# Attention with routed experts on one core: query and output products of most pairs in three passes of high and low parts

## The chip, the cores and the metric

One NeuronCore of a Trainium2 chip runs the whole program. The metric is the device time of one launch in microseconds, lower is better. 0.5% of it is 2.3 us.

## What is computed

The reference is a layer of cross attention followed by a routed feed-forward layer, for 2 sequences of 1024 tokens with 256 features and a context of 154 keys:

```
x = x + attention(layernorm(x), ctx)        # 16 heads of 16; q = xn Wq + bq, k, v from ctx
                                            # concat(softmax(q k^T / 4) v) Wo + bo
x = x + experts(layernorm(x))               # 8 experts, the best 2 per token, weighted by
                                            # softmax of the router's logits; gelu, 256 -> 1024 -> 256
```

All data is float32. The router's choice of 2 from 8 hangs on the attention's result, so products are kept at full or nearly full float32 accuracy.

## The kernel before

The 2048 tokens are 16 tiles of 128 rows, taken two at a time as 8 **pairs** (`MACROS = 8`, `PAIR = 256` columns). The attention stage is a software pipeline written out by hand: each engine has its own program of steps m = 0 to 7 (`step`, `quiet_step` for the last two, `QUIET = 6`, `LAST = 7`), and runs it strictly in that order; engines meet at semaphores (`wait_ge`, `then_inc`). In step m TensorE computes the scores of pair m + 2 (for their maxima), the scores of pair m again with keys on the partitions (`turned_scores`, ten per pair), the value sums, back transposes, head transposes and output product of pair m - 1, the router of pair m - 2, and the transposes and query product of pair m + 4. A pair's way through the engines:

- `statistics1` on VectorE and `next_norm1` on GpSimd normalise it; `xn_transposes` (L1441) turns it into a PSUM bank, `evac_xnT` on ScalarE (L654) copies it to `xnT`, `q_product` (L1450) multiplies by `wq_sb` into the same bank, `evac_q` (L661, L669) scales it and makes the rounded high part, `low_queries` on GpSimd (L487) the low part. Both go through DRAM (`qd`) into `QS` by DMAs that SP writes and GpSimd's queue reads (`queries_read`, L505).
- `scores` (L1483), `maxima` on VectorE (L1004), `negatives` (L1015, L1017), `maxima_transposes` (L1498). From pair 3 on these transposes wait until the residual sums of two pairs earlier are made.
- `turned_scores` (L1529, L1532), `exp` on ScalarE (L684), `value_sums` (L1555, L1557), `back_transposes` (L1567), `normalise` on VectorE (L1023, L1027), `head_transposes` (L1574) into `ps_a`, `evac_heads` on ScalarE (L696) to `OT`, `wo_product` (L1583) once per tile, `add_residual` on VectorE (L1037), `statistics2`, `norm2` on GpSimd, the transposes and `router`.

A `turned_scores` waits for the exponential two before it, since there are two banks. In step 1 VectorE and ScalarE also lay out the keys of the second sequence (`low_keys`, L978; `high_keys`, L732). In steps 6 and 7 the maxima are done, and VectorE starts on the routing: `places`, `slots_of` (L1211, L1213) and `lanes_of` (L1204) for the first 8 tiles in step 6, `choose(1)` and `sum_up(1)` (L1164 to L1261) for tiles 8 to 11 in step 7. These stand ahead of `add_residual`. On TensorE `ranks(1)` (L1621 to L1626) waits for `sum_up(1)` and stands ahead of the value sums of the last pair; `value_sums` of pair 6 wait for the first residual sum of pair 5.

Two kinds of products occur. On float32 tiles the multiplication is at full accuracy; on tiles of the 4-byte rounded type (`f32r`) one pass is made on rounded operands, and accuracy comes from splitting an operand into a rounded high part and the rounded rest. The expert stage does so already (`up`, L1832, three passes), with VectorE making low parts (L1361). `q_product` and `wo_product` are of the first kind:

```
last = mm(query_bank(m)[:, g * PAIR:(g + 1) * PAIR], wq_sb[:, c, g * P:(g + 1) * P],
          xnT[:, c, :], start=c == 0, stop=c == KC - 1)
```

## Time and profile before

| | |
|---|---|
| median of 3 runs | 454.18 us (453.14 to 455.15) |
| the profiled execution | 454.41 us, its span 452.5 us |
| busy over the span | TensorE 88%, weight loads 74%, VectorE 62%, ScalarE 51%, GpSimd 44% |
| mean granted TensorE clock | 0.944 |
| attention stage, routing, expert stage | to about 190 us, to about 210 us, to the end |

The profile is that of one execution. Times inside it are counted from the start of the span; engines other than the one that is looked at work at the same time. A TensorE record's duration is modelled and overlaps the next one's, so what a product costs is read from the chain of waits, where pieces don't overlap, or from the distance of starts. PEclk is the granted clock as a share of 2.4 GHz. In the rows below PE is TensorE, PEld its weight loads, DVE is VectorE, ACT ScalarE, POOL GpSimd.

### The profile page before, as it was taken

What the parts mean: (1) busy time and instruction counts of PE and PEld (TensorE: products, weight loads), DVE (VectorE), ACT (ScalarE), POOL (GpSimd) and SP (SyncE); (2) the same over time, 40 slices, a digit from 0 to 9 for tenths busy, and PEclk for the clock granted to TensorE, in tenths of its full rate; (3) what the DMA queues carried; (4) which work ended last, traced back from release to release, by engine and by line L of the source; (5) the groups of instructions that cost most, each with busy time, mean ns of one, the idle gap of its engine ahead of it and who ended that gap; (6) DMA issues with size and microseconds to landing.
All of it is one profiled execution on the core that took longest, in us unless ns stands there. A gap on an engine that the chain in (4) does not pass through costs nothing.

```text
span 452.5 us, 8680 instructions
## 1 busy us (share of the span) xinstructions
PE 400.3 (88%) x2742; PEld 334.0 (74%) x2743; DVE 279.1 (62%) x655; ACT 229.1 (51%) x420; POOL 199.8 (44%) x183
## 2 busy tenths in 40 slices
PE   6967798999999998658899999999999989999950
PEld 2645665768668665535899999999999979999940
DVE  2898848456475657786976646644468865744320
ACT  1653647456454664241756456544457755644420
POOL 4846567372632322006235363255434664452230
PEclk9895999999998999858999999999999999999995
DMA  8446553433610110753554542723227732232220
GB/s 236 138 101 138 120 118 80 97 97 73 167 40 16 54 48 30 252 172 94 219 182 102 180 62 56 212 48 50 44 47 220 215 65 48 44 54 30 25 29 12
DMA packets 25750, 45.39 MB, mean 100 GB/s; under 512 B 6512, under 2 KB 19952, under 8 KB 22960
## 3 DMA queue, kind: packets, MB, share of 16 engines
q0 software_dynamic: 8448, 15.77, 19.2%
q1 hardware_dynamic: 13760, 26.32, 18.3%
q10 hardware_dynamic: 3504, 2.83, 2.0%
q8 instruction: 20, 0.33, 0.3%
q14 instruction: 18, 0.15, 0.1%
HBM read 31.52 MB, written 13.39 MB: 99 GB/s over the span
## 4 chain that ended last, share of the span: by engine, by line
PE 69%; DVE 12%; DMA 5%; issue 4%; ACT 3%; POOL 1%; POOLq 0%; ACTq 0%; DVEq 0%
PE ps_s L1832 20%; PE ps_t L1849 14%; PE ps_t L1852 7%; DMA result<-big,rowtok 4%; DVE mx L1004 3%; PE ps_s L1483 3%; PE ps_t L1532 2%; PE ps_a L1557 2%; PE ps_c L1557 2%; PE ps_a L1555 2%; PE ps_c L1814 2%; PE ps_t L1529 2%; DMA big<-rows,gtok 2%; PE ps_c L1555 2%; PE ps_c L1450 1%
## 5 line engine op out<-in xcount | busy, mean ns | idle before, releaser
L1832 PE MATMUL ps_s<-xgT,KB 128*128 128x256 f32 x912 | 110.8, 280 | 3.0 <-DVE xgT L1361 3.0
L622 POOL DMA_INDIRECT result<-big,rowtok x38 | 63.6, 1673 | 111.4 <-DMA result<-big,rowtok 61.0
L1832 PEld LDWEIGHTS ps_s<-xgT,KB 128*128 128x128 f32 x912 | 108.5, 188 | 4.2 <-DVE xgT L1361 1.7
L1004 DVE TENSOR_REDUCE mx<-ps_s 128x4 f32<-128x616 f32 x64 | 49.4, 797 | 31.7 <-PE ps_s L1483 31.5
L590 POOL DMA_INDIRECT big<-rows,gtok x38 | 44.9, 1181 | 32.7 <-DVE gtok L1318 14.9
L1849 PE MATMUL ps_t<-KB,HTb 128*128 x160 | 56.9, 397 | 0.0
L684 ACT ACTIVATE big<-ps_t 128x512 f32<-128x512 f32 x80 | 45.3, 593 | 21.9 <-PE ps_t L1532 18.2
L1849 PE MATMUL ps_t<-KB 128*128 x144 | 51.9, 402 | 0.0
L876 ACT ACTIVATE big<-ps_t,wrow 128x256 f32<-128x256 f32 x38 | 18.1, 477 | 65.8 <-PE ps_t L1852 60.7
L1377 DVE TENSOR_TENSOR HTb<-big,HTb 128x512 fp32r<-128x512 f32 x40 | 27.6, 692 | 31.7 <-ACT big L868 31.6
L868 ACT ACTIVATE big<-ps_s 128x512 f32<-128x512 f32 x76 | 45.4, 597 | 0.0
L1852 PE MATMUL ps_t<-KB,HTb 128*128 x160 | 44.7, 280 | 0.0
L1852 PE MATMUL ps_t<-KB 128*128 x144 | 40.4, 281 | 0.0
L1377 DVE TENSOR_TENSOR KB<-big,KB 128x512 fp32r<-128x512 f32 x36 | 24.7, 692 | 24.7 <-ACT big L868 23.1
L1483 PE MATMUL ps_s<-KB 96*128 96x308 f32 x128 | 33.6, 356 | 6.2 <-DVE mx L1004 2.9
L452 POOL TENSOR_TENSOR mv<-mv,half_sb 128x2 f32<-128x2 f32 x15 | 11.1, 743 | 62.2 <-DVE mv L1048 45.0
L866 ACT ACTIVATE HTb<-ps_s 128x512 fp32r<-128x512 f32 x40 | 24.0, 601 | 26.1 <-PE ps_s L1832 23.9
L1409 DVE SCALAR_TENSOR_TENSOR big<-ps_t,wrow,big 128x256 f32<-128x256 f32 x38 | 17.8, 482 | 30.2 <-ACT big L876 21.6
L1849 PEld LDWEIGHTS ps_t<-KB,HTb 128*128 128x128 f32 x160 | 30.1, 188 | 6.6 <-issue 0.2
L1532 PE MATMUL ps_t<-KB 100*128 100x256 f32 x128 | 29.6, 327 | 4.2 <-ACT big L684 3.9
L1849 PEld LDWEIGHTS ps_t<-KB 128*128 128x128 f32 x144 | 27.1, 188 | 6.2
L1483 PEld LDWEIGHTS ps_s<-KB 96*128 96x128 f32 x128 | 21.5, 207 | 12.9 <-DVE mx L1004 6.2
(234 smaller groups left out, 714.2 us busy)
## 6 DMA issues: line engine op xcount, KB each, us to landing
VP<-in_wexp SPq DMA_DIRECT2D x8, 1024.0 KB
big<-in_wexp SPq DMA_DIRECT2D x8, 1024.0 KB
qd<-big SPq DMA_DIRECT2D x28, 128.0 KB, 2.3
KB<-qd POOLq DMA_DIRECT2D x7, 512.0 KB, 5.2
result<-x SPq DMA_DIRECT2D x8, 256.0 KB, 2.9
rows<-xn SPq DMA_DIRECT2D x8, 256.0 KB, 2.9
KB<-qd POOLq DMA_DIRECT2D x7, 256.0 KB, 5.4
XS<-in_x ACTq DMA_DIRECT2D x1, 1024.0 KB, 5.5
```

The costliest lines, as they stand in the source:

```text
L590: pool.indirect_dma_start(XG[:, n, :], None, rows, bass.IndirectOffsetOnAxis(gtok[:, n:n + 1], 0)).then_inc(xg_loaded[u % 2], 16)
L622: pool.indirect_dma_start(out, bass.IndirectOffsetOnAxis(rowtok[:, u, h:h + 1], 0), ys[:, 2 * (u % 2) + h, :], None, compute_op=ALU.add).t ...
L684: act.activation(dst, ps_t[(n + 1) % 2][:, :].rearrange("p (h n) -> p h n", h=2), ACT.Exp).then_inc(p_made, 1)
L866: act.activation(hidT[u % 2][:, 0, 2 * b:2 * b + 2, :], ps_s[b // 2][:, b % 2, :].rearrange("p (j n) -> p j n", j=2), ACT.Gelu)
L868: act.activation(hid[:, b, :], ps_s[b // 2][:, b % 2, :], ACT.Gelu).then_inc(hid_made, 1)
L1004: dve.tensor_reduce(mx[:, i, :, 2 * k:2 * k + 2].rearrange("p a b -> p b a"), ps_s[n % 2][:, :, 0:2 * KEYS].rearrange("p b (h k) -> p b h ...
L1377: dve.tensor_tensor(hidT[u % 2][:, 1, js, :], hid[:, b, :].rearrange("p (j n) -> p j n", j=2), hidT[u % 2][:, 0, js, :].bitcast(fp32), ALU ...
L1483: last = mm(ps_s[n % 2][:, j, 0:2 * KEYS], QS[0:96, u, p, i * P:(i + 1) * P], KS[0:96, b, p, :], start=True, stop=True)
L1532: last = mm(bank[:, h, :], KS[0:100, b, place(j - 2), h * KEYS:h * KEYS + P], QS[0:100, u, place(j - 2), :], start=True, stop=True)
L1832: last = mm(ps_s[j // 4][:, j // 2 % 2, (j % 2) * PAIR:(j % 2 + 1) * PAIR], w1[:, w, k, j * P:(j + 1) * P], xgT[:, u % 2, a, k, :], start= ...
L1849: mm(ps_t[h][:, :].rearrange("p (w d) -> p w d", w=2), hidT[u % 2][:, 0, j, half_rows], w2[:, bass.ds(par, 1), :, j, :].squeeze(1), start= ...
L1852: last = mm(ps_t[h][:, 0:D], hidT[u % 2][:, 1, j, half_rows], w2[:, bass.ds(par, 1), 0, j, :].squeeze(1), start=False, stop=j == HJ - 1, s ...
```

## The change

Three things. The weights `wo_sb` and `wq_sb` are split once into a rounded high part and a rounded rest, by GpSimd, early in the program. For pairs 4 to 7 of the query product and pairs 0 to 6 of the output product, ScalarE's copy out of PSUM now writes the rounded part, VectorE subtracts it from the same bank to make the low part (`low_xnT`, `low_heads`), and TensorE makes three passes: high by high, high by low, low by high. The remaining pairs are as before. The new tiles lie in `HTb`, which the expert stage uses later. And the order is changed at four places: `turned_scores(m, 5)` ahead of the query product, `exp(m, 5)` ahead of `evac_q`, in step 1 `high_keys(1, 2)` with it, and in steps 6 and 7 `turned_scores` 8 and 9 each one place forward, ahead of an output product. The diff, without declarations of semaphores:

```diff
@@ -134,6 +134,10 @@
+        HTb = sb("HTb", [P, HT], f32r)
+        OT2, xnT2, wo2, wq2 = (HTb[:, 1024 * n:1024 * n + 1024].rearrange("p (s c n) -> p s c n", s=2, c=KC) for n in range(4))
+        THREE = ((0, 0), (0, 1), (1, 0))
...
@@ -549,11 +554,19 @@
             low_queries(1)
+            pool.wait_ge(ld_w, 48)
+            pool.tensor_copy(wo2[:, 0, :, :], wo_sb[:, :, :]).then_inc(wo2_hi, 1)
+            pool.wait_ge(wo2_hi, 1)
+            pool.tensor_tensor(wo2[:, 1, :, :], wo_sb[:, :, :], wo2[:, 0, :, :].bitcast(fp32), ALU.subtract).then_inc(wo2_made, 1)
             queries_read(1)
             low_queries(2)
             next_norm1(3)
             queries_read(2)
             maxima_read(0)
+            pool.wait_ge(ld_q, 16)
+            pool.tensor_copy(wq2[:, 0, :, :], wq_sb[:, :, :]).then_inc(wq2_hi, 1)
+            pool.wait_ge(wq2_hi, 1)
+            pool.tensor_tensor(wq2[:, 1, :, :], wq_sb[:, :, :], wq2[:, 0, :, :].bitcast(fp32), ALU.subtract).then_inc(wq2_made, 1)
             next_norm1(4)
             low_queries(3)
...
@@ -651,7 +664,7 @@
-                act.activation(xnT[:, :, :], query_bank(m)[:, :].rearrange("p (c n) -> p c n", c=KC), ACT.Copy).then_inc(xnT_made, 1)
+                act.activation((xnT if m < RING else xnT2[:, 0, :, :])[:, :, :], query_bank(m)[:, :].rearrange("p (c n) -> p c n", c=KC), ACT.Copy).then_inc(xnT_made, 1)
@@ -693,7 +706,7 @@
-                act.activation(OT[:, :, :], ps_a[:, :].rearrange("p (g n) -> p g n", g=GROUPS), ACT.Copy).then_inc(OT_made, 1)
+                act.activation(OT2[:, 0, :, :], ps_a[:, :].rearrange("p (g n) -> p g n", g=GROUPS), ACT.Copy).then_inc(OT_made, 1)
@@ -821,6 +834,10 @@
                     exp(m, 4)
                 if m == 1:
                     high_keys(1, 0)
+                if has(0):
+                    exp(m, 5)
+                if m == 1:
+                    high_keys(1, 2)
                 if has(4):
                     evac_q(m + 4)
...
                 if has(0):
-                    for j in range(5, 10):
+                    for j in range(6, 10):
                         exp(m, j)
-                        if m == 1 and j in (5, 7):
-                            high_keys(1, (j - 1) // 2)
+                        if m == 1 and j == 7:
+                            high_keys(1, 3)
@@ -1026,6 +1043,16 @@
+            def low_xnT(m):
+                dve.wait_ge(xnT_made, m + 1)
+                dve.tensor_tensor(xnT2[:, 1, :, :], query_bank(m)[:, :].rearrange("p (c n) -> p c n", c=KC),
+                                  xnT2[:, 0, :, :].bitcast(fp32), ALU.subtract).then_inc(xnT_lo, 1)
+
+            def low_heads(m):
+                dve.wait_ge(OT_made, m + 1)
+                dve.tensor_tensor(OT2[:, 1, :, :], ps_a[:, :].rearrange("p (g n) -> p g n", g=GROUPS),
+                                  OT2[:, 0, :, :].bitcast(fp32), ALU.subtract).then_inc(OT_lo, 1)
@@ -1119,7 +1146,11 @@
                 if has(5):
                     statistics1(m + 5)
+                if has(4):
+                    low_xnT(m + 4)
                 for n in range(5, 8):
+                    if n == 7 and has(-1):
+                        low_heads(m - 1)
                     if has(2):
                         maxima(m + 2, n)
@@ -1445,8 +1476,16 @@
             def q_product(m, gs=range(GROUPS)):
                 if 0 in gs:
                     pe.wait_ge(xnT_made, m + 1)
+                    if m >= RING:
+                        pe.wait_ge(xnT_lo, m - RING + 1)
+                        pe.wait_ge(wq2_made, 1)
                 for g in gs:
                     for c in range(KC):
+                        if m >= RING:
+                            for k, (a, w) in enumerate(THREE):
+                                last = mm(query_bank(m)[:, g * PAIR:(g + 1) * PAIR], wq2[:, w, c, g * P:(g + 1) * P],
+                                          xnT2[:, a, c, :], start=c == 0 and k == 0, stop=c == KC - 1 and k == 2)
+                            continue
@@ -1579,7 +1618,15 @@
                 pe.wait_ge(OT_made, m + 1 + i * int(m == LAST))
...
+                if m < LAST:
+                    pe.wait_ge(OT_lo, m + 1)
+                    pe.wait_ge(wo2_made, 1)
                 for g in range(GROUPS):
+                    if m < LAST:
+                        for k, (a, w) in enumerate(THREE):
+                            last = mm((ps_a, ps_c)[i][:, 0:D], OT2[:, a, g, i * P:(i + 1) * P], wo2[:, w, g, :],
+                                      start=g == 0 and k == 0, stop=g == GROUPS - 1 and k == 2)
+                        continue
@@ -1723,10 +1770,10 @@
                 turned_scores(m, 7)
+                turned_scores(m, 8)
                 wo_product(m - 1, 0)
-                turned_scores(m, 8)
+                turned_scores(m, 9)
                 wo_product(m - 1, 1)
-                turned_scores(m, 9)
@@ -1773,10 +1820,10 @@
+                if has(0):
+                    turned_scores(m, 5)
                 if has(4):
                     q_product(m + 4)
-                if has(0):
-                    turned_scores(m, 5)
```

In step 3 TensorE's part from the head transposes (L1574, in the new program L1613) to the last scores of keys, before:

```order
L1574 MATMUL ps_a<-id_sb,heads 128x128 x4
L1532 MATMUL ps_t<-KB 128x256 x2
L1483 MATMUL ps_s<-KB 128x308 x2
L1450 MATMUL ps_c<-xnT,wq_sb 128x256 x4
L1529 MATMUL ps_t<-KB 128x256 x4
L1483 MATMUL ps_s<-KB 128x308 x2
L1583 MATMUL ps_a<-wo_sb,OT 128x256 x2
L1532 MATMUL ps_t<-KB 128x256 x2
L1583 MATMUL ps_c<-wo_sb,OT 128x256 x2
L1532 MATMUL ps_t<-KB 128x256 x6
```

and now, where the query product's three passes are L1486, the output product's L1627, and the scores of keys L1568 and L1571:

```order
L1613 MATMUL ps_a<-id_sb,heads 128x128 x4
L1571 MATMUL ps_t<-KB 128x256 x2
L1522 MATMUL ps_s<-KB 128x308 x2
L1568 MATMUL ps_t<-KB 128x256 x4
L1486 MATMUL ps_c<-HTb 128x256 x12
L1522 MATMUL ps_s<-KB 128x308 x2
L1627 MATMUL ps_a<-HTb 128x256 x6
L1571 MATMUL ps_t<-KB 128x256 x2
L1627 MATMUL ps_c<-HTb 128x256 x6
L1571 MATMUL ps_t<-KB 128x256 x6
```

The scores with the two key remainders (x4) have moved ahead of the query product, whose 4 products became 12; each output product went from 2 to 6.

VectorE in step 7, from the heads' normalisation (L1023, L1027) over the copy of the logits (L1110) to the first operations of the choice, before:

```order
L1023 RECIPROCAL rec<-ps_a 128x16
L1027 TENSOR_TENSOR heads<-ps_a,rec 128x256
L1023 RECIPROCAL rec<-ps_c 128x16
L1027 TENSOR_TENSOR heads<-ps_c,rec 128x256
L1110 COPY LG<-ps_s 128x16
L1164 TENSOR_REDUCE r_m<-LG 128x4
L1165 TENSOR_TENSOR r_b<-LG,r_m 128x32
L1166 TENSOR_TENSOR r_b<-r_b,em_sb 128x32
L1167 TENSOR_REDUCE r_c<-r_b 128x4
```

and now (L1040, L1044, L1137, and the choice from L1195 on):

```order
L1040 RECIPROCAL rec<-ps_a 128x16
L1044 TENSOR_TENSOR heads<-ps_a,rec 128x256
L1040 RECIPROCAL rec<-ps_c 128x16
L1044 TENSOR_TENSOR heads<-ps_c,rec 128x256
L1137 COPY LG<-ps_s 128x16
L1054 TENSOR_TENSOR HTb<-ps_a,HTb 128x512
L1195 TENSOR_REDUCE r_m<-LG 128x4
L1196 TENSOR_TENSOR r_b<-LG,r_m 128x32
L1197 TENSOR_TENSOR r_b<-r_b,em_sb 128x32
L1198 TENSOR_REDUCE r_c<-r_b 128x4
```

The subtraction for the low part of the heads (L1054) stands between the copy of the logits and the choice of the experts, ahead of all of it.

TensorE in the same step, from the head transposes to the rank products (L1621 to L1626), before:

```order
L1574 MATMUL ps_a<-id_sb,heads 128x128 x4
L1532 MATMUL ps_t<-KB 128x256 x2
L1583 MATMUL ps_a<-wo_sb,OT 128x256 x2
L1532 MATMUL ps_t<-KB 128x256 x2
L1583 MATMUL ps_c<-wo_sb,OT 128x256 x2
L1532 MATMUL ps_t<-KB 128x256 x2
L1621 MATMUL ps_s<-r_pick,before_bf 128x32
L1623 MATMUL ps_s<-r_sum_bf,ones_bf 128x32
L1626 MATMUL ps_s<-r_pick,ones_bf 128x24
L1626 MATMUL ps_s<-r_pick,ones_bf 128x16
L1626 MATMUL ps_s<-r_pick,ones_bf 128x8
```

and now (rank products L1668 to L1673):

```order
L1613 MATMUL ps_a<-id_sb,heads 128x128 x4
L1571 MATMUL ps_t<-KB 128x256 x4
L1627 MATMUL ps_a<-HTb 128x256 x6
L1571 MATMUL ps_t<-KB 128x256 x2
L1627 MATMUL ps_c<-HTb 128x256 x6
L1668 MATMUL ps_s<-r_pick,before_bf 128x32
L1670 MATMUL ps_s<-r_sum_bf,ones_bf 128x32
L1673 MATMUL ps_s<-r_pick,ones_bf 128x24
L1673 MATMUL ps_s<-r_pick,ones_bf 128x16
L1673 MATMUL ps_s<-r_pick,ones_bf 128x8
```

One score of keys has moved ahead of each output product; the rank products still come behind both.

## Rows read from the trace of the kernel before

**Rows 1.** Page, part 1: busy us (share of the span) xinstructions

```profile
PE 400.3 (88%) x2742; PEld 334.0 (74%) x2743; DVE 279.1 (62%) x655; ACT 229.1 (51%) x420; POOL 199.8 (44%) x183
```

**Rows 2.** Windows: us, PE, PEld, DVE, ACT, POOL busy (x), PEclk, DMA share, GB/s

```profile
96.30:114.50 18.20, 17.44 (x129) 13.40 (x127) 10.29 (x22) 9.93 (x19) 7.36 (x8) 1.00 0.42 103
...
130.90:148.90 18.00, 17.13 (x117) 13.03 (x115) 11.09 (x30) 8.29 (x15) 7.53 (x7) 0.91 0.11 34
...
72.00:77.00 5.00, 3.51 (x18) 2.22 (x17) 4.81 (x13) 4.78 (x9) 2.56 (x3) 1.00 0.28 70
...
77.00:80.70 3.70, 3.70 (x22) 1.27 (x21) 0.68 (x1) 0.22 (x1) 3.54 (x4) 0.54 0.43 131
...
142.00:145.70 3.70, 3.70 (x18) 3.64 (x18) 2.09 (x4) 1.77 (x4) 0.00 (x0) 0.54 0.00 0
```

**Rows 3.** Chain of waits in order of time: start us, us, what

```profile
108.64 1.73 PE ps_c L1450 x8
...
127.56 0.87 PE ps_a L1583 x4
...
162.14 0.43 PE ps_a L1555 x2
...
174.99 0.03 PE ps_s L1621
...
227.94 5.63 PE ps_s L1832 x48
```

**Rows 4.** One line's instructions: duration ns min/median/max, first and last start us, forms

```profile
L1361 DVE TENSOR_TENSOR xgT<-ps_c,xgT x19: 690/691/693, 210.2 to 413.0; 128x512 fp32r<-128x512 f32 x19
...
L519 POOL CAST KB<-big x4: 603/607/742, 17.8 to 19.8; 32x512 fp32r<-32x512 f32 x4
...
L487 POOL TENSOR_TENSOR big<-qf,big x8: 1257/1272/1499, 16.2 to 112.0; 128x512 fp32r<-128x512 f32 x8
```

**Rows 5.** Timeline of GpSimd, start: start us, us, line, operation [idle before <-releaser]

```profile
29.99 0.80 POOL L505 DMA_DIRECT2D KB<-qd  x1 [4.39 <-DMA qd<-big]
...
42.08 0.72 POOL L452 TENSOR_TENSOR mv<-mv,half_sb 128x2 f32<-128x2 f32 x1 [2.14 <-DVE mv L936]
```

**Rows 6.** Timeline of ScalarE, step 4

```profile
126.31 0.60 ACT L696 ACTIVATE OT<-ps_a 128x512 f32<-128x512 f32 x1 [0.65 <-PE ps_a L1574]
```

**Rows 7.** Timeline of VectorE and GpSimd, steps 0, 1 and 4

```profile
52.50 1.50 DVE L1004 TENSOR_REDUCE mx<-ps_s 128x4 f32<-128x616 f32 x2
...
73.29 1.26 POOL L487 TENSOR_TENSOR big<-qf,big 128x512 fp32r<-128x512 f32 x1
...
73.39 1.21 DVE L1017 SCALAR_TENSOR_TENSOR nm<-mx,nm 128x32 fp32r<-128x32 f32 x1
...
75.14 0.42 DVE L1037 TENSOR_TENSOR x<-ps_a,XS 128x256 f32<-128x256 f32 x1
...
128.65 0.19 DVE L1017 SCALAR_TENSOR_TENSOR nm<-mx,nm 128x32 fp32r<-128x32 f32 x1
```

**Rows 8.** Timeline of GpSimd, step 3

```profile
112.05 1.28 POOL L487 TENSOR_TENSOR big<-qf,big 128x512 fp32r<-128x512 f32 x1 [8.80 <-ACT big L669]
```

**Rows 9.** Timeline of VectorE, step 4

```profile
126.83 1.56 DVE L1004 TENSOR_REDUCE mx<-ps_s 128x4 f32<-128x616 f32 x2 [0.17 <-PE ps_s L1483]
```

**Rows 10.** Timeline of ScalarE and VectorE, step 6

```profile
158.29 0.28 DVE L1211 TENSOR_TENSOR o_code<-r_o,pick_code 128x128 f16<-128x128 f32 x1
...
159.03 0.59 ACT L696 ACTIVATE OT<-ps_a 128x512 f32<-128x512 f32 x1
...
159.06 1.23 DVE L1204 TENSOR_TENSOR XS<-count_sb,lane_f 128x1024 f16<-128x1024 f32 x1
```

**Rows 11.** Timeline of VectorE and ScalarE, step 7

```profile
171.25 0.19 DVE L1164 TENSOR_REDUCE r_m<-LG 128x4 f32<-128x32 f32 x1
...
171.87 0.59 ACT L696 ACTIVATE OT<-ps_a 128x512 f32<-128x512 f32 x1
...
174.55 0.17 DVE L1261 CAST r_sum_bf<-r_sum 128x8 bf16<-128x8 f32 x1
```

More of the change, by code:

```diff
@@ L210, in xattn_moe_kernel @@
         hid = big[:, o5:o5 + HID * 2].rearrange("p (b n) -> p b n", b=4)
-        HTb = sb("HTb", [P, HT], f32r)
         hidT = [part.rearrange("p (s j n) -> p s j n", s=2, j=HJ)
@@ L246, in xattn_moe_kernel @@
         v_psum, v_made = sem("v_psum"), sem("v_made")
+        xnT_lo, OT_lo, wo2_hi, wo2_made, wq2_hi, wq2_made = (sem(n) for n in
+            ("xnT_lo", "OT_lo", "wo2_hi", "wo2_made", "wq2_hi", "wq2_made"))
         st1_made, mv1_made, var1_made, rstd1_made = (sem(n) for n in ("st1_made", "mv1_made", "var1_made", "rstd1_made"))
```

## The prediction

> **What bounds the kernel now.** The change lies in the attention stage (before 190 us), so I began with the page's totals and went on to the stretches of that stage. Over the span TensorE is busy 88%, VectorE 62% [rows 1]: on average VectorE has room. By steps (step m scores pair m, prepares pairs m + 1 to m + 5 and finishes pairs m - 1 and m - 2) TensorE is busy 17.44 of 18.20 us in step 3 and 17.13 of 18.00 in step 5 [rows 2]. It sets the pace, and it waits for a few tenths wherever a result of ScalarE or VectorE is just in time. Twice its granted clock is down at half (1.2 of 2.4 GHz) for some 3.7 us: the rows 77 to 80.7 and 142 to 145.7 show a mean of 0.54 [rows 2]. Each costs up to 1.8 us. The chain of waits runs through TensorE nearly without a break; so an instruction that TensorE loses is a gain only if nothing else comes late, and a late operand is a loss at its full length.
>
> **Products.** A 4-byte product of 256 columns is two records of 0.216 us: the query product (4 products) 1.73 us, one output product (2 products) 0.87 us [rows 3]. A product of rounded operands is one record: 48 of them take 5.63 us, 0.117 each, with the same 128x128 weights and 256 columns [rows 3]. New query product: 12 x 0.117 = 1.41, 0.32 less, four times: -1.3 us. New output product: 6 x 0.117 = 0.70, 0.17 less, fourteen times: -2.3 us. Full credit would be **-3.6 us**.
> The Trainium skill (FP8 and Floating Point Precision, TensorE Precision Notes) counts a true FP32 product as four passes through the array. Three of four would be 1.30 and 0.65 us, and -4.8 us in all; the rows speak for less, since a pass that is an instruction of its own takes 0.117 and not 0.108.
>
> **ScalarE** writes the rounded part in place of the 4-byte copy: same shape, same 0.6 us [rows 6], nothing.
>
> **GpSimd splits the weights.** A cast of 512 elements a lane takes 0.60 to 0.74 us, a subtraction of two SBUF tiles 1.26 to 1.50 [rows 4]: 1.9 to 2.2 us per split. The first stands where GpSimd idles 4.39 us for a transfer, the second where it idles 2.14 us for VectorE [rows 5]. Both are covered; the second just so, and what is queued behind it (the norm of pair 4, then pair 3's low query part) has more than a microsecond left. I take 0 and keep +0.7 as the upper end: a cast that gets in ahead of VectorE's first norm would hold it that long.
>
> **VectorE's low parts.** Eleven subtractions, PSUM minus SBUF, 128x512, rounded on output. The nearest row is the same operation of the expert stage: 0.69 us [rows 4]. VectorE works in its program's order, so their cost is where they stand and what is queued behind them. I go step by step.
> Steps 0 and 1 are already full on VectorE. In step 0 the low part stands in front of the maxima that ran at 52.50 [rows 7]; it ends at about 53.2, TensorE wanted the query product at 52.4 (the moved scores of keys cover 0.5), so the product ends 1 us later. ScalarE's exponential 5, now ahead of the query evacuation, gives most of it back: **+0.2**. In step 1 1.4 us are added to a VectorE that is busy 4.81 of the 5 us from 72 to 77 [rows 2]. Before, 1.0 us of it was lost anyway: L1017 took 1.21 us, where it takes 0.19 in step 4, until GpSimd's L487 had ended [rows 7]. But two low parts push the third key copy (L978) into the same stretch of GpSimd; it then waits in L1017's place, and itself, L1015, L1017, the last copy still stand between it and the residual sum. That sum moves from 75.14 to about 76.0, and the transposes of the maxima wait for it: **+0.9** (0.1 if GpSimd comes second).
> The Trainium skill (SBUF — State Buffer, Who interferes with whom) says that a copy or cast in a two-port mode, or an operation with two SBUF inputs against a reading GpSimd, waits for the whole instruction of the other, while one with a single SBUF input does not. L1017 agrees. By it the new subtractions themselves stay at 0.69 beside GpSimd, and it is the copies around them that pay.
> Step 2: the query product waits 0.3 for its low part and the output product 0.4, against 0.65 saved; ScalarE, with the last key copies, is the bound at the end: **+0.1**. Step 3 has no statistics, and both low parts come in time. TensorE saves 0.65, but with the scores moved ahead the query product ends when it did, so GpSimd's L487 still starts at 112.05 and ends at 113.33 [rows 8]; L1017 waits for that as before, and the residual sum behind it holds the next transposes: **-0.2**.
> Step 4 has no query product. ScalarE's copy of the turned heads ends at 126.91 [rows 6], but VectorE was taking the last two maxima of the step, 126.83 to 128.39 [rows 9]; the low part goes between them, 127.6 to 128.3. TensorE was at the output product at 127.56 [rows 3]; it now starts at 128.35 with its first weight load not covered (0.2). Loss 1.0, less 2 x 0.17 saved: **+0.65**. Step 5 is the same, but in this execution half its work ran at half clock, which gave VectorE time: **+0.4**.
> Step 6: the scores of keys put ahead of the output product cover the low part (copy ends 159.62, low part 160.3). Behind it on VectorE stand the slot tables and the lane table (0.7 + 1.23 us), which ran from 158.29 to 160.29 while the heads were under way [rows 10]. Now they run from 160.35 to 162.4, then comes the residual sum of pair 5, 162.75, and the next value sums wait for it; they began at 162.14 [rows 3]: **+0.7**.
> Step 7 is the largest. VectorE chose the experts of tiles 8 to 11 from 171.25 to 174.72, 17 small operations without a gap [rows 11], in the shadow of ScalarE's copy at 171.87 and of the output products. The low part now stands ahead of them and can't start before 172.46, when the copy ends; it ends at 173.16. The choice ends at 173.2 + 3.47 = 176.65. TensorE's rank products wait for its sum, and the value sums of the last pair are queued behind them. They started at 174.99, with 0.2 us in hand [rows 3]; now at 176.8: **+1.8**. Nothing later has slack for it up to the first expert product.
> Sum: 0.2 + 0.9 + 0.1 - 0.2 + 0.65 + 0.4 + 0.7 + 1.8 = **+4.55 us**. The profiled execution took 454.41 us (span 452.5); that makes 459.0. The median of the three runs is 454.18, so the sum would be 458.7 against it; I stay with 459.0. The expert stage is untouched.
>
> **The range.** Adding the lower ends (start 0, steps 0, 0.1, -0.2, -0.5, 0.5, 0, 0.5, 1.7) gives +2.1, the upper ones (0.7, then 0.5, 1.0, 0.4, 0, 0.8, 0.7, 0.8, 2.0) +6.9. One stretch of half clock less or more moves either end by 1.8: 454.7 to 463.1, of which I keep 454.7 to 462.5, since all upper ends together are unlikely.
>
> **Rivals.**
> (1) *The passes pay in full.* If the new waits all fall into time in which TensorE would wait anyway, the -3.6 us stand, less a little: 451 us. For it: TensorE is the bound in steps 3 to 5. Against it: the ends of the copies and the starts of the products are in the rows, and step 7's 17 operations have nowhere to go. The point from which it decides is where the low part ends before TensorE has reached the output product; only step 3 is there. Chance 0.08.
> (2) *The clock stays up.* If both stretches of half clock disappear, since the work of steps 1 and 5 falls otherwise, 3.6 us come back: 4.55 - 3.6, 455.4, within 0.5%. For it: in the rows it went down after stretches with short waits, and other steps with such waits kept it. Chance 0.14.
> (3) *The new waits bring more half clock.* In step 7 TensorE would stand still for nearly 2 us and then start the value sums. Before the drop at 77 it had stood still 1.5 of 5 us, in pieces [rows 2]. One to two stretches more give +1.8 to +3.6: 461 to 462.6. Chance 0.14.
> The Trainium skill (TensorE: Matmul & The Clock Gate, What's actually happening) has the throttled state as the default that activity releases; that is on the side of (3).
> (4) *The change does not do what it says*, the products not taking the one-record form: then twelve records would be 24 and the query product 5.2 us; since the tiles are declared in the same type as those of rows 3, I give it nothing of its own.
>
> **Chances.** The queue losses of the sum as they stand 0.64, (3) 0.14, (2) 0.14, (1) 0.08. A measurement of this kernel can tell about 0.5%, 2.3 us, from no change: slower is above 456.5, faster below 451.9. The sum's own case falls below 456.5 in one of ten. Slower 0.58 + 0.14 + a little of (2) = 0.76, same 0.17, faster 0.07. The range 454.7 to 462.5 leaves out (1), the far end of (3) and a little of (2), some 0.17.
>
> **What would show it.** Right: output product records of half the length, near 0.28 busy with 0.117 between them; TensorE waits for the new VectorE line ahead of the output product of pairs 3 and 4, about 0.8 us each; in step 7 a gap of nearly 2 us ahead of the rank products, released by VectorE's sum; the value sums of pair 6 starting on the residual sum. Wrong: no gap there, or the new VectorE line at more than 0.8 us, or an expert stage that starts no later than now.

## The result and the profile after

The changed kernel takes 458.24 us, median of five runs (457.81 to 459.24); the kernel before, beside it, 453.25 (452.39 to 455.15). The ratio is 1.0103, with a 95% interval of 1.0067 to 1.0139: 3.0 to 6.3 us slower. Forecast were 459.0 and "slower". The profiled execution of the changed kernel took 458.24 us with a span of 456.3. Medians here are of all runs; the ratios, and the fit further down, leave out nine of 207 runs that were over 1.5% slower than the fastest of their kernel.

Page of the changed kernel, part 1, against [rows 1]:

```profile
PE 401.4 (88%) x2786; PEld 335.5 (74%) x2787; DVE 282.7 (62%) x666; ACT 229.0 (50%) x420; POOL 206.5 (45%) x187
```

VectorE has its eleven instructions and GpSimd its four; TensorE is as busy as before over the span. That sum hides what happened in the steps, so the next thing to read is a window for each step, against [rows 2]: steps 4 and 5, the old place of half clock at 142, and the two new ones. The first line is step 4 of the kernel before, the others are the changed kernel.

```profile
114.40:130.80 16.40, 15.53 (x117) 11.45 (x115) 10.12 (x25) 8.19 (x16) 7.13 (x11) 1.00 0.46 114
...
114.00:131.10 17.10, 15.43 (x120) 11.38 (x118) 10.24 (x24) 8.17 (x16) 7.12 (x11) 1.00 0.49 112
131.10:148.30 17.20, 15.55 (x121) 11.47 (x120) 11.56 (x31) 8.27 (x16) 7.52 (x7) 1.00 0.11 35
142.00:145.70 3.70, 2.87 (x21) 2.65 (x22) 3.54 (x5) 2.01 (x4) 0.00 (x0) 1.00 0.00 0
159.90:163.60 3.70, 3.66 (x16) 3.43 (x16) 2.41 (x5) 1.03 (x4) 0.00 (x0) 0.55 0.01 2
187.20:190.90 3.70, 3.25 (x8) 2.00 (x6) 2.63 (x12) 0.00 (x0) 0.57 (x1) 0.55 1.00 407
```

In step 4 TensorE is busy 15.43 us instead of 15.53, but the step takes 17.1 us instead of 16.4: what was added is waiting. The granted clock (third number from the end) fell to half in other places than before: near 58, at 159.9 and at 187.2, and no longer at 77 and 142. So step 5 looks faster than before (17.14 against 17.99) and step 6 looks slower than it is.

Timeline of TensorE in the changed kernel, the new products:

```profile
52.80 1.66 PE L1486 MATMUL ps_c<-HTb 128*128 128x256 f32 x12 [0.69 <-issue]
...
74.26 0.95 PE L1627 MATMUL ps_a<-HTb 128*128 128x256 f32 x6 [1.54 <-DVE HTb L1054]
...
127.96 0.95 PE L1627 MATMUL ps_a<-HTb 128*128 128x256 f32 x6 [0.78 <-issue]
128.75 0.40 PE L1571 MATMUL ps_t<-KB 100*128 100x256 f32 x2
128.98 0.87 PE L1627 MATMUL ps_c<-HTb 128*128 128x256 f32 x6
129.69 0.52 PE L1571 MATMUL ps_t<-KB 100*128 100x256 f32 x3
...
177.16 0.19 PE L1668 MATMUL ps_s<-r_pick,before_bf 128*128 128x32 bf16 x1 [0.80 <-DVE r_pick L1207]
177.20 0.18 PE L1670 MATMUL ps_s<-r_sum_bf,ones_bf 128*128 128x32 bf16 x1
```

From the chain of waits of the changed kernel, against L1450 and L1583 in [rows 3]:

```profile
52.80 1.67 PE ps_c L1486 x12
...
109.33 1.44 PE ps_c L1486 x12
...
111.05 0.72 PE ps_a L1627 x6
...
127.96 0.95 PE ps_a L1627 x6
```

In step 3, where TensorE doesn't wait, a query product takes 1.44 us in the chain instead of 1.73, an output product 0.72 instead of 0.87: the credit of 0.3 and 0.15 is there, at about 0.12 us a pass. Behind a wait it is gone or nearly so: the query product of step 0 takes 1.67 us and the first output product of step 4 takes 0.95 (the forecast had 0.2 us there for a first weight load that nothing covers). Ahead of the first output product of steps 4 to 7 stands an idle time of 0.76 to 0.78 us, in step 1 one of 1.54. "issue" in the timeline doesn't say whom it waited for; the end of VectorE's low part does:

```profile
23.09 2.04 DVE L1084 TENSOR_SCALAR xn<-XS,mv 128x256 f32<-128x256 f32 x2
...
52.01 0.68 DVE L1049 TENSOR_TENSOR HTb<-ps_c,HTb 128x512 fp32r<-128x512 f32 x1
...
74.75 0.99 DVE L995 CAST KB<-big 32x616 fp32r<-32x616 f32 x1
...
76.72 0.42 DVE L1064 TENSOR_TENSOR x<-ps_a,XS 128x256 f32<-128x256 f32 x1
...
127.18 0.68 DVE L1054 TENSOR_TENSOR HTb<-ps_a,HTb 128x512 fp32r<-128x512 f32 x1
...
159.15 0.69 DVE L1054 TENSOR_TENSOR HTb<-ps_a,HTb 128x512 fp32r<-128x512 f32 x1 [1.28 <-ACT HTb L709]
...
160.53 1.22 DVE L1235 TENSOR_TENSOR XS<-count_sb,lane_f 128x1024 f16<-128x1024 f32 x1
161.67 0.42 DVE L1064 TENSOR_TENSOR x<-ps_a,XS 128x256 f32<-128x256 f32 x1
...
173.68 0.69 DVE L1054 TENSOR_TENSOR HTb<-ps_a,HTb 128x512 fp32r<-128x512 f32 x1 [1.28 <-ACT HTb L709]
174.28 0.17 DVE L1195 TENSOR_REDUCE r_m<-LG 128x4 f32<-128x32 f32 x1
...
176.92 0.18 DVE L1207 TENSOR_TENSOR r_pick<-r_o 128x32 bf16<-128x32 f32 x1
...
177.59 0.17 DVE L1292 CAST r_sum_bf<-r_sum 128x8 bf16<-128x8 f32 x1
```

This is VectorE of the changed kernel in the start and in steps 0, 1, 4, 6 and 7. 127.18 + 0.68 is 127.86, and the product starts at 127.96. In step 7 VectorE stands idle for 1.28 us for ScalarE's copy, does the low part, and only then begins the choice of the experts (at 174.28; in [rows 11] the choice began at 171.25, ahead of the copy). Its picks are ready at 177.10, and the rank products start at 177.16.

### The profile page after: what moved, and what is told of

Read it like the earlier page. It is cut to its first block, busy times and chain, and to the rows that moved or that the text cites. A ratio compares the mean times of both kernels' runs of the same rounds, so it can differ in the third digit from the quotient of the medians.

```text
span 456.3 us, 8801 instructions
## 1 busy us (share of the span) xinstructions
PE 401.4 (88%) x2786; PEld 335.5 (74%) x2787; DVE 282.7 (62%) x666; ACT 229.0 (50%) x420; POOL 206.5 (45%) x187
## 4 chain that ended last, share of the span: by engine, by line
PE 64%; DVE 10%; DMA 9%; issue 6%; POOL 4%; ACT 3%; ACTq 0%; SPq 0%; DVEq 0%; POOLq 0%
PE ps_s L1879 18%; PE ps_t L1896 12%; PE ps_t L1899 6%; PE ps_s L1522 3%; DMA big<-rows,gtok 3%; PE ps_t L1571 3%; DMA result<-big,rowtok 2%; DVE mx L1021 2%; PE ps_a L1596 2%; PE ps_a L1594 2%; PE ps_t L1568 2%; PE ps_c L1596 2%; PE ps_t L1457 2%; PE ps_c L1594 2%; PE ps_c L1861 2%
## 5 line engine op out<-in xcount | busy, mean ns | idle before, releaser
L635 POOL DMA_INDIRECT result<-big,rowtok x38 | 64.6, 1699 | 108.7 <-DMA result<-big,rowtok 63.2
L603 POOL DMA_INDIRECT big<-rows,gtok x38 | 46.9, 1235 | 33.1 <-DVE gtok L1349 14.6
L1896 PEld LDWEIGHTS ps_t<-KB,HTb 128*128 128x128 f32 x160 | 30.0, 188 | 6.3 <-issue 0.2
L1571 PE MATMUL ps_t<-KB 100*128 100x256 f32 x128 | 27.1, 309 | 3.7 <-ACT big L697 3.7
L1899 PEld LDWEIGHTS ps_t<-KB,HTb 128*128 128x128 f32 x160 | 30.2, 189 | 0.0
```

Of the source, the lines that this page charges most:

```text
L603: pool.indirect_dma_start(XG[:, n, :], None, rows, bass.IndirectOffsetOnAxis(gtok[:, n:n + 1], 0)).then_inc(xg_loaded[u % 2], 16)
L635: pool.indirect_dma_start(out, bass.IndirectOffsetOnAxis(rowtok[:, u, h:h + 1], 0), ys[:, 2 * (u % 2) + h, :], None, compute_op=ALU.add).t ...
L1571: last = mm(bank[:, h, :], KS[0:100, b, place(j - 2), h * KEYS:h * KEYS + P], QS[0:100, u, place(j - 2), :], start=True, stop=True)
L1896: mm(ps_t[h][:, :].rearrange("p (w d) -> p w d", w=2), hidT[u % 2][:, 0, j, half_rows], w2[:, bass.ds(par, 1), :, j, :].squeeze(1), start= ...
L1899: last = mm(ps_t[h][:, 0:D], hidT[u % 2][:, 1, j, half_rows], w2[:, bass.ds(par, 1), 0, j, :].squeeze(1), start=False, stop=j == HJ - 1, s ...
```

## The lengths of the steps

To follow one step through many kernels I measured in every profile from the first maxima transpose of one step to that of the next; step 6 ends at the value sums of pair 6, step 7 at the rank products. A number with * has 3.2 to 3.4 us at half clock in it, which lengthens it by up to half of that. The lengths of the other experiments stand in their text.

| step | before | before again | after | order only | no low parts | low parts early | low part ahead of maxima 6 | low part in the middle |
|---|---|---|---|---|---|---|---|---|
| 0 | 11.85 | 11.86 | 12.24 | 11.62 | 11.35 | 11.35 | 12.26 | 13.50* |
| 1 | 18.52 | 19.17 | 20.20* | 18.03 | 18.88 | 19.78 | 20.58* | 18.63 |
| 2 | 20.15* | 20.09* | 18.81 | 18.44 | 19.64* | 19.57* | 18.81 | 18.82 |
| 3 | 18.17 | 18.14 | 17.56 | 18.17 | 17.59 | 17.55 | 17.57 | 17.57 |
| 4 | 16.43 | 16.42 | 17.14 | 16.42 | 17.69* | 16.53 | 16.55 | 18.31* |
| 5 | 17.99* | 16.43 | 17.14 | 16.43 | 17.65* | 17.69* | 16.55 | 17.16 |
| 6 | 13.20 | 13.21 | 14.80* | 12.97 | 12.65 | 13.49 | 13.97 | 13.48 |
| 7 | 12.85 | 12.86 | 14.09 | 12.62 | 12.29 | 13.04 | 14.08 | 13.03 |

Where no half clock is in it and GpSimd doesn't collide with VectorE (all but step 1), a step of the same work repeats to 0.04 us from profile to profile. The totals don't: the runs of the kernel before spread from 450.6 to 460.0 us, and about two thirds of that variance goes with the granted clock. I therefore also fitted 198 runs by least squares with one constant for each kernel and one price, the same for all kernels, for a microsecond at half clock. That price came out at 0.26 us (+-0.02), and the constants, all at 45 us of half clock, stand with the experiments as "at equal clock" (standard error 0.3 to 0.5 us, 0.1 for before): 454.1 for before, 457.5 for after.

## The experiments

My theory: each loss is a place in VectorE's queue, and moves with the low part. The rivals: the order moves or GpSimd's weight splits cost the time; or the clock does, and then nothing done to the queue gives it back. Each kernel below has 6 to 12 runs, but for the repeat of before, which has one. The kernel before took 454.69 us beside one to four, 453.73 beside five to eight and 455.99 beside nine to twelve.

**One: the last two steps as before** (three passes for the output products of pairs 0 to 4 only, and the scores of steps 6 and 7 in their old order).

```
+        WIDE = 5
...
-                if m < LAST:
+                if m < WIDE:
                     pe.wait_ge(OT_lo, m + 1)
```

> Steps 6 and 7 as in the kernel before (4-byte output products of pairs 5 and 6, old order, no low part on VectorE there); steps 0 to 5 as changed. Theory (low parts stand in VectorE's queue ahead of routing work): the stretch from the maxima transposes of step 5 to the rank products of step 7 falls back from 28.9 to about 26.1 us, and the whole to 455.5 to 456.5 us against 458.2 of the change. Rival (the loss comes from steps 0 to 5 or from half clock alone): stays at 457.5 to 458.5.

Measured: 458.23 us, ratio 1.0088 (1.0054 to 1.0121); at equal clock 456.4, 1.1 under the change. Steps 6 and 7 came back to 13.21 and 12.86, those of before. The total missed my expectation and lies where the rival had it. The profile shows 17.1 us at half clock before step 0 where the change had 13.7, which at the fitted price is 0.9 us; the steps speak for the queue, the total alone for neither.

**Two: the query products alone** (no output product in three passes; the scores of steps 6 and 7 in their old order).

```
+        WIDE = 0
...
-                if m < LAST:
+                if m < WIDE:
                     pe.wait_ge(OT_lo, m + 1)
```

> Only the query products of pairs 4 to 7 in three passes; all output products 4-byte, no low part of the heads; both weights still split by GpSimd, order of steps 0 to 3 as changed. Theory: the query side is nearly even (steps 0 and 1 lose some tenths, step 3 gains 0.3), 453.0 to 454.5 us against 453.3 before. Rival (weights' split and the query side carry a good part of the loss): 455 to 456 us.

Measured: 457.86 us, ratio 1.0051 (1.0014 to 1.0089); at equal clock 455.0. Steps 4 and 5 are 16.43 and 16.43 again. The total is above both expectations, with on average 51 us at half clock against 47 for before, and step 1 took 21.95 us with 6.8 at half clock.

**Three: the low part of pair 5 between slot tables and lane table, that of pair 6 in the middle of the choice.**

```
                     slots_of(0)
+                    low_heads(m - 1)
                     lanes_of(0, 0)
...
+                if n == 1:
+                    low_heads(LAST - 1)
```

> As the change, but in step 6 the low part of the heads stands between slot tables and lane table, in step 7 in the middle of the choice of the experts. Theory: VectorE no longer stands idle for the copy (1.28 us twice); the picks are 0.7 us late, within the slack of 0.9 us that TensorE had there, so the gap ahead of the rank products goes, 1.2 us less in step 7 and 0.3 to 0.7 in step 6: 456.3 to 457.0 us. Rival (the passes and the low part's own 0.69 us are what costs): 457.8 to 458.5.

Measured: 457.86 us, ratio 1.0075 (1.0047 to 1.0103); at equal clock 457.0. Step 6 fell from 13.97 (its length without half clock, in four) to 13.48, step 7 from 14.09 to 13.03. The total is above what I expected, in the rival's range. TensorE waits for the low part just as long, but the gap ahead of the rank products is gone:

```profile
176.73 0.95 PE L1630 MATMUL ps_a<-HTb 128*128 128x256 f32 x6 [0.76 <-issue]
...
178.46 0.19 PE L1671 MATMUL ps_s<-r_pick,before_bf 128*128 128x32 bf16 x1
```

The gap of 0.80 us ahead of the rank products was due to what is queued behind the low part.

**Four: in steps 4 and 5 the low part ahead of the last two maxima.**

```
-                    if n == 7 and has(-1):
+                    if n == (6 if m in (4, 5) else 7) and has(-1):
```

> As the change, but in steps 4 and 5 the low part of the heads stands ahead of maxima 6 and not behind them. Theory: it ends 0.6 to 0.7 us earlier, TensorE's wait ahead of the output product (0.78 us) shrinks to 0.1 to 0.2, steps 4 and 5 take 16.5 us in place of 17.1: 1.2 us less, 457.0 us. Rival (ScalarE's exponentials bound these steps anyway): no change, 458.2.

Measured: 458.43 us, ratio 1.0115 (1.0066 to 1.0163); at equal clock 457.2. Steps 4 and 5 fell from 17.14 to 16.55. Its TensorE timeline has 0.18 us where 0.78 stood:

```profile
127.78 0.96 PE L1627 MATMUL ps_a<-HTb 128*128 128x256 f32 x6 [0.18 <-issue]
```

The total didn't show the 1.2 us of the two steps: the median is that of the change, where I expected 457.0, and at equal clock only 0.3 of them appear, with an error of 0.5 us on either kernel. In the steps the low part's place is shown to cost 0.6 us each; in the total it can't be told.

**Five: all low parts early** (the places of three; in steps 1 to 5 the place of four; and the low query part ahead of the statistics).

```
-                if has(5):
-                    statistics1(m + 5)
                 if has(4):
                     low_xnT(m + 4)
                 for n in range(5, 8):
-                    if n == 7 and has(-1):
+                    if n == 6 and has(-1) and m < QUIET:
                         low_heads(m - 1)
+                    if n == 7 and has(5):
+                        statistics1(m + 5)
```

> The change with every low part placed where VectorE has room: low_xnT ahead of statistics1, low_heads of steps 1 to 5 ahead of the maxima of strip 6, the one of step 6 between the slot tables and the lane table, the one of step 7 in the middle of the choice of the experts. My theory (each loss is a queue position on VectorE) expects steps 4 and 5 at 16.5 us instead of 17.1, the stretch of step 6 at 13.5 and that of step 7 at 13.0, the start of step 0 to step 1 no longer than 12.2 and step 1 at 18.5 to 19.2 without half clock, so 2.5 to 3 us less than the change at the same clock: 455 to 456.5. The rival that the loss sits in the clock, not in the queue, expects the same shorter steps and a total within 1 us of the change, with more us at half clock. The rival that the passes pay in full once nothing is late expects 451 to 452.

Measured: 456.28 us, ratio 1.0046 (1.0016 to 1.0076); at equal clock 455.1, 2.4 (+-0.6) less than the change. The steps are as expected but for step 1 (19.78). Most of the loss at equal clock is gone, at the same three passes, the same eleven subtractions and the same splits. The rival "the passes pay in full" found no support: with the low parts at these better places the kernel is still no faster than before. In one, three, four and five the totals at equal clock give back 1.1, 0.5, 0.3 and 2.4 us of the 2.0, 1.5, 1.2 and about 3.7 that their steps became shorter (steps 1 and 2 left out, and step 5 of five taken like step 4). All four are counted from the same five runs of the change, with an error of 0.5 us, so whether a part is lost again elsewhere stays open.

**Six: the weight splits alone** (before, plus GpSimd's four instructions; nobody reads what they write).

```
             low_queries(1)
...
+            pool.tensor_copy(wo2[:, 0, :, :], wo_sb[:, :, :]).then_inc(wo2_hi, 1)
...
+            pool.tensor_tensor(wo2[:, 1, :, :], wo_sb[:, :, :], wo2[:, 0, :, :].bitcast(fp32), ALU.subtract).then_inc(wo2_made, 1)
...
             maxima_read(0)
...
+            pool.tensor_copy(wq2[:, 0, :, :], wq_sb[:, :, :]).then_inc(wq2_hi, 1)
```

> The kernel before plus GpSimd's two weight splits alone; what they write is read by nobody, everything else is as before. My theory (the splits stand in GpSimd's idle time) expects no difference: 0 to 0.3 us, the maxima transposes of step 0 at 45.2 to 45.7 at the same clock, steps 0 and 1 at 11.85 and 18.5. The rival (the casts hold VectorE in the start, or the clock goes down for longer there) expects 0.7 to 3 us more, with the transposes of step 0 at 46.4 to 48.6, as three of the five kernels with splits showed.

Measured: 455.96 us, ratio 1.0030 (0.9996 to 1.0064); at equal clock 454.3, 0.2 over before. Nothing can be told from no change. All steps are within 0.03 us of those of before.

**Seven: three passes only where they gained** (query pairs 6 and 7, output pairs 1 and 2, which are steps 2 and 3; in these steps the low parts stand at the places of five, and all other steps have their old order; the splits stay early).

```
+        Q3, O3 = (6, 7), (1, 2)
...
-                        if m >= RING:
+                        if m in Q3:
```

> Three passes only where the traces show room on VectorE: query products of pairs 6 and 7 and output products of pairs 1 and 2, which fall into steps 2 and 3, with the order of those steps as in the change and of all others as before. My theory expects steps 0 and 1 as before (11.85 and 18.5), step 3 at 17.5 (0.6 less), step 2 at about 18.5 (0 to 0.3 less than its clean value), the rest as before: 0.6 to 1.2 us faster than before, 453. The rival that any three-pass product brings more time at half clock expects no gain, 454 to 456, with over 3 us more at half clock.

Measured: 453.09 us beside 453.73 for before, ratio 0.9951 (0.9914 to 0.9987); at equal clock 452.3. Step 3 is 17.55 and steps 4 to 7 are those of before. This is the one version that comes out ahead of the kernel before, by the ratio 0.5%. Its interval only just leaves out 1, the two medians are 0.6 us apart, and the same products with the splits elsewhere (nine) are no faster than before, so the 0.6 us of step 3 are sure and the total is not.

**Eight: the kernel before again**, for a second profile.

> The kernel before itself, for a second profile: the lengths of its steps where the clock falls elsewhere. Both theories expect a span of 450.5 to 455.5; step 1 at 18.5 and step 3 at 18.17 again if these are the clean values, and step 2 and step 5 at 18.3 to 18.5 and 16.4 to 16.5 if they are free of half clock this time.

Measured: 453.08 us, span 451.1. Step 5 is 16.43 without half clock, so [rows 2] had 1.56 us of clock in it. Step 1 is 19.17 us with no half clock either, 0.65 more than the first time: its length is not fixed even for one kernel.

**Nine: as seven, with the weight splits behind the low queries of pairs 3 and 4.**

```
             low_queries(3)
+            pool.wait_ge(ld_w, 48)
+            pool.tensor_copy(wo2[:, 0, :, :], wo_sb[:, :, :]).then_inc(wo2_hi, 1)
...
                     low_queries(m + 4)
+                if m == 0:
...
+                    pool.tensor_copy(wq2[:, 0, :, :], wq_sb[:, :, :]).then_inc(wq2_hi, 1)
```

> The kernel with three passes in steps 2 and 3 only (query pairs 6 and 7, output pairs 1 and 2), with GpSimd's two weight splits moved out of the start: the one of the output weights behind the low queries of pair 3, where GpSimd idles 3.92 us before 51.76, the one of the query weights behind those of pair 4 in step 0, where it idles 4.36 us before 63.65. My theory (the first cast holds VectorE's norm at 23 us, 2.02 us instead of 1.57) expects the norm back at 1.57, 0.3 to 0.6 us less in the start at the same clock, and 0 elsewhere: 452.3 to 452.8, 0.7 per cent under the kernel before. The rival (the norm was held by the low queries' subtraction and not by the cast, and the start is set by the clock) expects no change from the 453.1 of the early splits.

Measured: 456.95 us, ratio 1.0033 (0.9999 to 1.0067); at equal clock 454.2. My theory of this place fell: the norm took 1.83 us, not 1.57, and the kernel got slower, with step 0 at 14.20*. Timelines of this kernel in step 0, first VectorE:

```profile
49.75 1.58 DVE L984 TENSOR_SCALAR big<-big,mask 128x308 fp32r<-128x308 f32 x2
...
54.56 1.25 DVE L953 TENSOR_SCALAR mv<-mv 128x2 f32<-128x2 f32 x1
```

then GpSimd:

```profile
48.89 0.60 POOL L566 CAST HTb<-wo_sb 128x512 fp32r<-128x512 f32 x1
49.58 1.29 POOL L568 TENSOR_TENSOR HTb<-wo_sb,HTb 128x512 fp32r<-128x512 f32 x1
...
54.49 1.28 POOL L498 TENSOR_TENSOR XS<-XS,bo_sb 128x512 f32<-128x512 f32 x1
```

and the same masking where GpSimd is idle, in the kernel of experiment ten:

```profile
48.34 0.66 DVE L971 TENSOR_SCALAR big<-big,mask 128x308 fp32r<-128x308 f32 x2
```

An idle stretch of GpSimd is not free: VectorE's two masking operations took 0.92 us more beside the split. A tiny one of 0.17 took 1.25, beside a GpSimd addition (L498) that the kernel before has too, so the split only moved it there. TensorE waited 0.95 us for maxima behind the masking, a wait that the kernel of ten doesn't have (a later one of 0.81 it has as well), and from 54.4 on the clock was down, as the window shows:

```profile
54.40:58.10 3.70, 3.70 (x14) 3.10 (x13) 2.78 (x4) 0.78 (x2) 3.46 (x5) 0.54 0.94 188
```

That the added wait brought the clock down is my reading and not shown. In the first profile of before the clock fell at 142.0 too, where TensorE had waited only 0.16 and 0.26 us in the 5 us ahead of it.

**Ten: the order moves alone** (before, with scores and exponential 5 ahead of the query product and scores 8 and 9 ahead of the output products).

```
+                if has(0):
+                    turned_scores(m, 5)
                 if has(4):
                     q_product(m + 4)
-                if has(0):
-                    turned_scores(m, 5)
```

> The kernel before with nothing but the change's order moves: scores and exponential 5 ahead of the query product, the second high keys earlier, and in the last two steps scores 8 and 9 ahead of the output products. My theory (the moves cost 0 to 0.5 us by themselves; they only cover the low parts) expects every step within 0.3 us of before, step 1 within 0.5, and a total of 453.5 to 454.5. The rival that the moves, not the low parts, cost the time in the last two steps expects step 6 at 13.9 and step 7 at 14.0.

Measured: 454.02 us beside 455.99, ratio 0.9980 (0.9946 to 1.0014); at equal clock 454.0. Steps 0, 6 and 7 are each 0.23 us shorter than before. I had the moves down as cover with a price; in these steps they are a small gain, which the total doesn't show.

**Eleven: the change without the low parts** (the third pass takes the high part again).

```
-        THREE = ((0, 0), (0, 1), (1, 0))
+        THREE = ((0, 0), (0, 1), (0, 0))
...
-                    pe.wait_ge(OT_lo, m + 1)
```

> The change without VectorE's eleven low parts and the waits for them: the third pass of each product takes the high part again, so the three passes, the weight splits and the order stay, and the low parts of the activations are left out of the result. My theory (VectorE's queue is what costs) expects step 4 and step 5 at 16.1 to 16.4, step 6 at 13.0, the stretch of step 7 at 12.7, step 1 at 18.1 or less, the split of step 0 at 11.4, in all 5 to 6.5 us less than the change at the same clock: 451.5 to 453. The rival that the loss is more time at half clock, caused by shorter products or other weights, expects 455 or more with the steps short.

Measured: 474.79 us, ratio 1.0415 (1.0363 to 1.0466), which says nothing on the theory. This kernel doesn't only leave the low parts out, as I had put it: its third pass adds the product of the two high parts a second time, so these query and output products come out at about twice their size. The result is another one, tokens go to other experts, the expert stage gathers 42 tiles instead of 38 and takes 262.0 us instead of 241.5, and the total that I had expected can't be checked. The lengths of the steps can, since the attention stage has the same instructions whatever the values: 11.35, 17.59, 12.65 and 12.29 for steps 0, 3, 6 and 7. From the start of step 0 to the rank products it takes 127.74 us, 10.2 of them at half clock; the change takes 131.98, 6.8 at half clock.

**Twelve: as five, with both weight splits behind the low queries of pair 3.**

```
             low_queries(3)
...
+            pool.tensor_copy(wq2[:, 0, :, :], wq_sb[:, :, :]).then_inc(wq2_hi, 1)
...
+            pool.tensor_copy(wo2[:, 0, :, :], wo_sb[:, :, :]).then_inc(wo2_hi, 1)
```

> The whole change with the low parts placed early as in the fifth experiment, and both weight splits behind the low queries of pair 3 (query weights first), where GpSimd idles 3.92 us before 51.76 in the kernel before. My theory expects the norm in the start at 1.57 us, 0.3 to 0.6 us less in the start, no wait of the query product of pair 4 for its weights, and 455.7 to 456.1 in all, against 456.28 with the early splits. The rival (the splits have nothing to do with the start) expects 456.3 again.

Measured: 459.46 us, ratio 1.0103 (1.0069 to 1.0137), with 59.5 us at half clock on average against 50.6 in five; at equal clock 456.0. The expectation missed as in nine, and the same thing is seen twice over: the masking took 2.04 us instead of 0.66, and two stretches of half clock stand in the windows from step 0 on:

```profile
54.70:58.40 3.70, 3.68 (x18) 3.68 (x19) 3.02 (x8) 0.60 (x1) 1.99 (x3) 0.56 0.93 193
61.20:65.00 3.80, 3.80 (x18) 2.20 (x18) 0.80 (x1) 1.45 (x3) 1.15 (x1) 0.55 0.27 63
```

The Trainium skill (SBUF — State Buffer, Who interferes with whom) says that `copy`, `cast` and `tensor_scalar` on VectorE can enter two-port modes, and that whoever issues first then blocks the other for its whole instruction. By that rule L984 pays beside GpSimd and the subtraction from PSUM doesn't; the traces agree. L984 took 0.66 us with GpSimd idle and 1.58 and 2.04 beside it; the seven instructions of L1054 in the changed kernel took 677 to 692 ns, and the shortest, at 92.31, lies wholly beside GpSimd's norm.

## Why the prediction was right, and where it was not

The direction, the size (+4.55 forecast, 458.24 - 453.25 = +4.99 measured) and the kind of cause held. Single terms did not, and that the sum landed so near is in part luck: step 1 (0.8 too much by the lengths below), step 7 (0.6) and step 3 (0.4) were forecast too dear, steps 0, 2, 4 and 5 too cheap by 0.9 together, and the clock added the rest. Experiments ten and eleven split the net change of a step into what the order moves, the shorter products and the low parts do:

| step | before | order moves | passes | low parts | after | forecast |
|---|---|---|---|---|---|---|
| 0 | 11.85 | -0.23 | -0.27 | +0.89 | 12.24 | +0.2 |
| 3 | 18.17 | 0 | -0.58 | -0.03 | 17.56 | -0.2 |
| 6 | 13.20 | -0.23 | -0.32 | +1.32 | 13.97 (four) | +0.7 |
| 7 | 12.85 | -0.23 | -0.33 | +1.80 | 14.09 | +1.8 |

The +1.80 of step 7 is counted from the shorter 12.29; the forecast's +1.8 was a net term, and is to be held against 14.09 - 12.85 = +1.24.

- **Products.** Forecast 1.41 and 0.70, in the chain 1.44 and 0.72. Their credit arrives nearly whole where nothing is late: 0.58 of 0.65 us in step 3. The estimate from the four passes that the Trainium skill counts (FP8 and Floating Point Precision, TensorE Precision Notes) was 1.30 and 0.65, at 0.108 us a pass; the trace does not agree, with 1.44 and 0.72, at 0.120 a pass.
- **Step 0**, +0.4 instead of +0.2. The low part does hold the product: it ends at 52.69 and TensorE starts at 52.80, and behind that wait the product takes 1.67 us, not 1.41.
- **Step 1**, forecast +0.9: not confirmed. The wait that was forecast for the copy is in the trace of the changed kernel, where the third key copy (L995) takes 0.99 us at 74.75 instead of about 0.5, and the residual sum starts at 76.72 where before it started at 75.14. But the step's length is 18.5 and 19.2 in two profiles of before, 18.03 with the order moves alone and 18.63 with the whole change in experiment three. What the low parts add there is inside that spread; only experiment five, with 19.78 and no half clock, lies above it. The traces show one part of the spread. Where GpSimd's low query part catches the operation L1017, that takes about 1.2 us, and step 1 takes 18.5 to 19.2 us (before, before again, eleven); where it comes too late for that, the operation takes 0.22 and the step 18.03 and 18.09 (ten, seven). In three, as in the changed kernel, it catches the copy instead (1.01 us) and L1034 takes 0.19: the new stall stands in place of the old one, and the forecast added it nearly whole. The rest stays open.
- **Step 2**, 18.81 against 18.44 with the order moves alone: +0.4 instead of +0.1.
- **Step 3**, -0.6 instead of -0.2. The forecast had "L1017 waits for that as before", and this step failed. First row before, second row after:

```profile
112.22 1.15 DVE L1017 SCALAR_TENSOR_TENSOR nm<-mx,nm 128x32 fp32r<-128x32 f32 x1
...
112.14 0.19 DVE L1034 SCALAR_TENSOR_TENSOR nm<-mx,nm 128x32 fp32r<-128x32 f32 x1
```

GpSimd's subtraction started at 112.45, so this operation was ahead of it and didn't wait. Nor had the old wait held the step: in the kernel before, the chain of waits there runs through the output products and an exponential, not through VectorE.
- **Steps 4 and 5**, +0.71 each (17.14 against 16.43 without half clock). Forecast +0.65 and +0.4. The low part's place between maxima 6 and 7 was most of it: experiment four gives 0.6 of it back.
- **Step 6**, +0.77 in experiment four, free of half clock; forecast +0.7.
- **Step 7** is **the term that was mis-sized**: +1.24, not +1.8. VectorE was late as forecast: its choice began 9.27 us behind the value sums of pair 6 before and 11.21 after, 1.94 more (forecast 1.9). The slack was wrong. The prediction had "TensorE's rank products wait for its sum" with 0.2 us in hand, and so has the section on the kernel before. They don't: the first one waits for the picks (L1207), which stand three small instructions ahead of the last sum, as the releaser of L1668 shows; the second (L1670, 177.20) runs before that sum is cast (L1292, 177.59), since it takes the sum of the part before. In the kernel before the picks were ready at 173.89 + 0.18 = 174.07:

```profile
173.89 0.18 DVE L1176 TENSOR_TENSOR r_pick<-r_o 128x32 bf16<-128x32 f32 x1
...
174.83 0.19 PE L1621 MATMUL ps_s<-r_pick,before_bf 128*128 128x32 bf16 x1
```

That is 0.76 us in hand, of which 0.06 are left after the change: 1.94 - 0.70 = 1.24.
- **Start**, forecast 0 (up to +0.7): 0.2 +- 0.35 at equal clock in experiment six. VectorE's norm took 2.04 us in the changed kernel (first row of its VectorE above) and 1.57 in both profiles of before. It is not the split's cast that held it: that starts at 24.92, and the norm's two parts end 0.15 us behind GpSimd operations of the kernel before, its key casts (23.61) and its low query part (24.98). The stretch before step 0 took 45.2 to 48.6 us in all profiles and its clock (10.2 to 17.1 us at half) explains only a part. What sets it was not found.

The steps sum to 0.4 + 0.1 + 0.4 - 0.6 + 0.7 + 0.7 + 0.8 + 1.2 = +3.7 us (step 1 taken from experiment three against the first profile of before), and the fit at equal clock gives +3.4. So the forecast's +4.55 was about one microsecond too much as a sum of queue losses. The interval of the measured difference, 3.0 to 6.3 us, holds both. A part of the difference is clock: the profiled run of the changed kernel has a granted clock of 0.941 where that of before has 0.944, 3.2 us more at half clock. One stretch of it, at 187.2, makes the last output products take 1.86 and 1.91 us for 1.13 and 1.03 before, and the stretch from the rank products to the first expert product 1.15 us longer. That is the part of rival (3) that came true; that the landing is within 0.8 us of 459.0 is owed in part to it.

Of the rivals: (1) is out by the measured time and by five; (2), the two stretches of half clock going away, happened at their places and was made up elsewhere; (3), more half clock, came as less than one stretch in the changed kernel (1.7 us on the mean of the fitted runs) and as some three to four in twelve; (4) did not occur, since twelve passes take 1.44 us in the chain.

## What to carry to other kernels

A cheaper instruction on the bound engine pays only where its new operand has time to be made. Ask first what is queued behind the maker: here 0.69 us of VectorE cost 1.8 us once, 1.3 us once and nothing in step 3, and moving the low parts a few places gave back 2.4 of 3.4 us. Take such a change only in the steps where it gains; and before you put work into an idle stretch of GpSimd, look at what VectorE does in it.

## What was not expected of the hardware

- Idle time of GpSimd was not free for VectorE: a pair of masking operations of 0.66 us took 1.58 and 2.04 beside a cast and a subtraction of 128x512, and a 128x2 operation 1.25 instead of 0.17 beside a 128x512 addition.
- Stretches of half clock come back at other places when the waits move. Kernels that differ little have on average 45 to 46 (seven, ten) to 59.5 us (twelve) at half clock; each us of it costs 0.26 us of the total in the fit, less than the half that it would cost if TensorE were the bound all the time. A saving of 1.2 us in two steps (experiment four) can vanish in that.
- Moving independent scores, 0.5 us of them in step 0 and 0.24 in steps 6 and 7, ahead of a product that waits, with nothing else changed, made three steps 0.23 us shorter each.
